# Turning gathered expert rows by transposing DMAs instead of TensorE transposes

## The chip, the cores and the metric

The kernel runs on one core of a Trainium2 chip. The metric is the device time of one execution, in microseconds. Engines are called TensorE (PE in the rows, PEld for its weight loads), VectorE (DVE), ScalarE (ACT), GpSimd (POOL) and SyncE (SP, whose queue issues plain DMAs). Each has its own queue of instructions, worked off in order, and they meet only through semaphores.

## The reference

Input x is (8, 1024, 256) in float32. An attention layer comes first, then a layer of 16 experts in which each expert picks its 1024 best tokens (expert choice), plus a shared expert:

```python
x = x + layernorm(attention(layernorm(x)))
h = layernorm(x)                                 # 8192 rows of 256
scores = softmax(h @ gate_w.T).T                 # 16 x 8192
topk_weight, topk_idx = top_k(scores, 1024)
xg = h[topk_idx]                                 # 16 x 1024 x 256, gathered rows
hid = gelu(xg @ Wg.T) * (xg @ Wu.T)              # 1024 hidden values
eo = (hid @ Wd.T) * topk_weight                  # scattered back by addition
shared = (gelu(h @ Sg.T) * (h @ Su.T)) @ Sd.T    # 512 hidden values, all rows
x = x + layernorm(scatter_add(eo) + shared)
```

## The kernel before, in words

After the attention (the first 615 us) all of the expert layer is one list of blocks of 512 rows, which every engine goes through in the same order (schedule, L1377). Blocks 0 to 11 are three quarters of the shared expert's rows, blocks 12 to 43 (E0 = 12, D0 = 44) are the 16 experts with two blocks each (tb = 0 and tb = 1, called even and odd here), and the last four are the rest of the shared expert.

An expert block has 8 steps (one for each 128 hidden values) and a down-projection. In a step TensorE does 12 matmuls of 512 columns (up, L1426): gate and up, two halves of the 256 features, each as three products of high and low parts (mm3, L57), since float32 values are split into two parts for the fast matmul. The order is

```python
for it in range(2, its[b]): step(b, it)
for it in range(2): step(b + 1, it)
down(b)
```

so step 0 of block b+1 follows step 7 of block b at once, and the down-projection of b (32 matmuls of 512 and 32 of 256 columns, 11.2 us) comes after step 1 of b+1.

What other engines do in a step: ScalarE (step, L1609) waits for TensorE's step, computes the gelu into HF (L1614), copies the high part of the hidden values of the step before (part_hi, L1578), and where there is one a quarter of a weight's high part (w_hi, L1555; wd in steps 4 to 7 of even blocks, the next expert's wg and wu in all steps of odd ones). VectorE (step, L1799) multiplies HF by the up-projection (L1802), then makes the low parts: of the hidden values (part_lo, L1723), of the weight (w_lo, L1712). In even blocks it also sums and centers rows of wd (L1746, L87) in steps 2 to 4. TensorE's step s waits until the product of step s-2 is done (s_mul). PSUM and HF have two buffers.

The input of a block is XT[b % 2], turned (features on partitions) and split into high and low part, each in two halves dk of 128 features. TensorE waits ahead of step 0 of block b for both low halves of it:

```python
if it == 0:
    wait(pe, s_xlo, 2 * (b + 1))
wait(pe, s_mul, s - 1)
```

For expert blocks x comes from gathered rows: GpSimd issues 8 indirect DMAs for each expert (gather, L2055; 128 rows each) into XG[n % 2], rows on partitions. TensorE turns the rows of block b+1 in steps 3 and 4 of block b, one half dk each with 4 transposes into PSUM (turn_part, L1412, L1423; semaphore s_xt). In the same steps, behind the weight, ScalarE takes the high part out of PSUM (x_hi, L1557, L1572) and VectorE the low part (x_lo, L1714, L1718; semaphore s_xlo). The first expert block is turned whole in step 3 of the last shared block. s_xt also tells GpSimd and SyncE when XG may be written again.

Of the kernel before, what the change touches and what calls it, by code (L numbers as in the profile page):

```python
# [23 lines left out]
F32 = mybir.dt.float32  # L24
F32R = mybir.dt.float32r
BF16 = mybir.dt.bfloat16
I32 = mybir.dt.int32
ALU = mybir.AluOpType
ACT = mybir.ActivationFunctionType
# [4 lines left out]
P = 128  # L34
E = 16
# [1231 lines left out]
def moe(nc, io, c):  # L1267
# [7 lines left out]
    with ExitStack() as ctx:  # L1275
# [46 lines left out]
        cm = new("cm", [P, NI])  # L1322

        def tile(u, t):
            b, first, _ = WHERE[u]
            return F[b][:, first + t, :]
# [22 lines left out]
        s_hlo2, s_evd = sem("s_hlo2"), sem("s_evd")  # L1349
        s_f = {u: sem(f"s_f_{u}") for u in ("d0", "d1", "e0", "e1", "e2", "e3", "e4", "e5", "b7")}  # L1350
        s_cen, s_sqv, s_sqa, s_r, s_pc, s_n, s_o = (sem(n) for n in ("s_cen", "s_sqv", "s_sqa", "s_r", "s_pc", "s_n", "s_o"))
# [3 lines left out]
        tail = Tail(io, c, sem, new, psG, psU, psX, psD)  # L1355
        tail.s_ev_down0, tail.ev_down0 = s_ev, EV0 + 4
# [46 lines left out]
        def _(pe):  # L1403
            def turn(b):

                n, tb = expert(b)
                q = n % 2
                wait(pe, s_ga[q][tb], 64 * (n // 2 + 1))
                for dk in range(KD):
                    turn_part(b, dk)  # L1410

            def turn_part(b, dk):  # L1412

                n, tb = expert(b)
                q = n % 2
                if dk == 0:
                    wait(pe, s_ga[q][tb], 64 * (n // 2 + 1))
                if b > E0:
                    wait(pe, s_xlo, 2 * (b - 1) + dk + 1)
                else:  # L1420
                    wait(pe, topk.s_acc, AHEAD)
                for t in range(4):
                    i = pe.transpose(psX[:, dk, t * P:(t + 1) * P], XG[q][:, 4 * tb + t, dk * P:(dk + 1) * P], c.ident[:, :])  # L1423
                i.then_inc(s_xt, 1)

# [10 lines left out]
            def step(b, it):  # L1436
                s = base[b] + it
                if is_b(b) and s % 4 == 3:
                    topk.sum(pe, s - 1.5 - SHIFT)
                if is_b(b):  # L1440
                    tail.p_begin(pe, s)
                if is_e(b):
                    n, tb = expert(b)
                    if tb == 0 and it % 2 == 0:
                        for w in "gu":
                            wait(pe, s_wlo[w], 4 * n + it // 2 + 1)
                if b == D0 and it == 0:
                    pe.wait_ge(s_dlo, 3)
# [4 lines that stand above are left out]
                def middle():  # L1453
                    if is_b(b):
                        if s % 4 == 0:
                            topk.sum(pe, s - 2 - SHIFT)
                        topk.tensor_at(pe, s - 0.25 - SHIFT)
                        tail.p_middle(pe, s)
                        if b == E0 - 1 and it == 3:
                            turn(E0)  # L1460

                if is_b(b):
                    up(it, XT[b % 2], (bsw["g"], bsw["u"]), middle)
                    topk.tensor_at(pe, s - SHIFT)
                    tail.p_end(pe, s)
                elif is_e(b):
                    up(it, XT[b % 2], (wg[n % 2], wu[n % 2]), middle)
                    if it in (3, 4) and is_e(b + 1):
                        turn_part(b + 1, it - 3)
                    if it == 6 and 0 <= b - 1 - E0 < NCH - AHEAD:  # L1470
                        topk.p_list(pe, AHEAD + b - 1 - E0)
                else:
                    up(it, XT[b % 2], (dsw["g"], dsw["u"]), middle)
# [65 lines left out]
        def _(a):  # L1539
# [17 lines left out]
            def x_hi(b, dk):  # L1557
                dst = XT[b % 2][0][:, dk, :]
                if is_b(b):
                    src = XR[b % 2][:, dk, :]  # L1560
                    if dk == 0:
                        wait(a, s_xr[b % 2], 16 * (b // 2 + 1))
                elif is_e(b):
                    src = psX[:, dk, :]
                    wait(a, s_xt, 2 * (b - E0) + dk + 1)
# [23 lines left out]
            def squares(u, ts):  # L1589

                for t in ts:
                    if u in ("d2", "d3"):
                        wait(a, s_evd, 4 * int(u[1]) + t + 1)
                    else:
                        wait(a, s_f[u], 16)
                    z = BASE[u] + t
# [12 lines left out]
            def step(b, it):  # L1609
# [7 lines left out]
                if is_b(b):  # L1617
# [90 lines left out]
        def _(v):  # L1708
# [5 lines left out]
            def x_lo(b, dk):  # L1714
                hi, lo = (t[:, dk, :] for t in XT[b % 2])
                src = XR[b % 2][:, dk, :] if is_b(b) else psX[:, dk, :] if is_e(b) else XRD[b - D0][:, dk, :]
                wait(v, s_xhi, 2 * b + dk + 1)
                v.tensor_tensor(lo, src, hi.bitcast(F32), ALU.subtract).then_inc(s_xlo, 1)  # L1718

            def part_lo(b, it):  # L1720
# [40 lines left out]
            def squares(u, ts):  # L1761

                if u[0] == "e":
                    wait(v, s_f[u], 16)
                v.drain()
# [33 lines left out]
            def step(b, it):  # L1799
# [16 lines left out]
                elif is_e(b):  # L1816
# [116 lines left out]
        def _(sp):  # L1933
# [68 lines left out]
            load_shared("d")  # L2002
            sp.wait_ge(s_xt, 4 * (E - 1))
            sp.wait_ge(s_tw, E - 1)
# [10 lines left out]
            load_shared("u")  # L2015
            sp.wait_ge(s_xt, 4 * E)
            sp.wait_ge(s_tw, E)
# [31 lines left out]
        def _(g):  # L2049
# [83 lines left out]
            part_lo(1, 1)  # L2133
            g.wait_ge(s_sqa, 1)
            chain(0)
# [17 lines left out]
            g.wait_ge(s_sqv, 6)  # L2153
            g.wait_ge(s_sqa, 2)
            chain(4)
            part_lo(3, 3)
            store("e2")
            g.wait_ge(s_sqa, 3)
            chain(5)
            g.wait_ge(s_sqa, 4)  # L2160
            chain(6)
# [68 lines left out]
```

## Time and profile before

| | us |
|---|---|
| median of 3 runs | 2064.74 |
| lowest, highest | 2063.34, 2065.69 |
| the profiled execution | 2064.56 |
| its span in the profile | 2062.6 |
| TensorE busy in the span | 2022.0 (98%) |
| VectorE, ScalarE, GpSimd busy | 1320.0, 970.5, 511.6 |

The span goes from the first to the last instruction of the profile. An engine's row in a timeline gives the start, the length and, in square brackets, how long the engine had been idle before it and what it had waited for. Lengths of neighbours overlap, as the engines are pipelined; what an instruction costs its queue is the distance from start to start.

### The profile page before, as it was taken

To read this page: it belongs to the slowest core of one execution; us is meant where nothing else is said; L and a number is where in the kernel's file an instruction comes from. 1 tells how busy PE (TensorE), PEld (TensorE's weight loads), DVE (VectorE), ACT (ScalarE), POOL (GpSimd) and SP (SyncE) were. 2 spreads that over 40 slices of the span, in tenths; PEclk is the share of its full clock that TensorE was granted. 3 is DMA by queue.
4 is the path that set the end of the run, shared out by engine and by line. 5 is a ranking of instruction groups with operands and counts; after the bars stand their busy time and mean duration, and the time that the engine had idled before them with its cause. 6 is when DMAs were issued, how large, how long until landed. Compare 5 with 4: busy or idle time off the path is not lost.

```text
span 2062.6 us, 30183 instructions
## 1 busy us (share of the span) xinstructions
PE 2022.0 (98%) x11290; PEld 1724.4 (84%) x11290; DVE 1320.0 (64%) x2489; ACT 970.5 (47%) x1840; POOL 511.6 (25%) x604
## 2 busy tenths in 40 slices
PE   7999999999999999999999999999999999999996
PEld 6888888888888888888888888888888888888885
DVE  6676686676667678666656666655555555555647
ACT  4564574564554444444434344444444444444444
POOL 0021022022021000314223332333233323322246
PEclk9999999999999999999999999999999999999998
DMA  3011111111015211333333333333332333234466
GB/s 115 1 42 43 62 63 42 61 62 46 38 68 191 84 62 52 98 81 65 91 63 74 78 71 83 81 74 72 83 83 73 70 85 83 73 70 116 105 211 163
DMA packets 56395, 163.96 MB, mean 79 GB/s; under 512 B 9552, under 2 KB 26064, under 8 KB 49104
## 3 DMA queue, kind: packets, MB, share of 16 engines
q1 hardware_dynamic: 30880, 124.55, 16.7%
q0 software_dynamic: 25392, 37.77, 11.5%
q8 instruction: 78, 1.28, 0.3%
q14 instruction: 45, 0.37, 0.1%
HBM read 102.97 MB, written 59.31 MB: 79 GB/s over the span
## 4 chain that ended last, share of the span: by engine, by line
PE 67%; DVE 2%; ACT 0%; DMA 0%; DVEq 0%; issue 0%; SPq 0%; ACTq 0%
PE mo_psD L1502 11%; PE mo_psG L59 7%; PE mo_psU L59 7%; PE mo_psU L60 7%; PE mo_psU L61 7%; PE mo_psG L61 7%; PE mo_psG L60 7%; PE mo_psD L1504 6%; PE mo_psD L59 2%; PE mo_psD L61 1%; PE mo_psD L60 1%; PE mo_psX L1423 1%; PE mo_psX L1228 1%; DVE mo_junk_v L1768 0%; DVE mo_HF L1802 0%; DMA X1a<-wd_in 0%
## 5 line engine op out<-in xcount | busy, mean ns | idle before, releaser
L1614 ACT ACTIVATE mo_HF<-mo_psG 128x512 f32<-128x512 f32 x320 | 191.3, 598 | 466.6 <-PE mo_psU L61 437.1
L1802 DVE TENSOR_TENSOR mo_HF<-mo_psU,mo_HF 128x512 f32<-128x512 f32 x320 | 220.6, 689 | 282.7 <-ACT mo_HF L1614 280.4
L2081 POOL DMA_INDIRECT ACC<-OUT,mo_GI x128 | 202.6, 1583 | 674.5 <-DVE OUT L1884 666.1
L1502 PE MATMUL mo_psD<-wd,mo_H_hi 128*128 128x512 f32 x1024 | 360.9, 393 | 0.2 <-DVE OUT L1884 0.2
L1504 PE MATMUL mo_psD<-wd,mo_H_lo 128*128 128x256 f32 x1024 | 289.4, 283 | 0.0
L59 PE MATMUL mo_psG<-mo_XT_hi,wg_hi 128*128 128x512 f32 x640 | 261.1, 408 | 2.3 <-DVE mo_HF L1802 1.8
L59 PE MATMUL mo_psU<-mo_XT_hi,wu_hi 128*128 128x512 f32 x640 | 253.3, 396 | 0.0
L61 PE MATMUL mo_psG<-mo_XT_hi,wg_lo 128*128 128x512 f32 x640 | 252.8, 395 | 0.0
L60 PE MATMUL mo_psU<-mo_XT_lo,wu_hi 128*128 128x512 f32 x640 | 252.6, 395 | 0.0
L61 PE MATMUL mo_psU<-mo_XT_hi,wu_lo 128*128 128x512 f32 x640 | 252.4, 394 | 0.0
L60 PE MATMUL mo_psG<-mo_XT_lo,wg_hi 128*128 128x512 f32 x640 | 252.3, 394 | 0.0
L1502 PEld LDWEIGHTS mo_psD<-wd,mo_H_hi 128*128 128x128 f32 x1024 | 192.3, 188 | 44.9 <-DVE OUT L1884 0.5
L1723 DVE TENSOR_TENSOR mo_H_lo<-mo_HF,mo_H_hi 128x512 fp32r<-128x512 f32 x304 | 207.7, 683 | 0.0
L1578 ACT ACTIVATE mo_H_hi<-mo_HF 128x512 fp32r<-128x512 f32 x318 | 198.5, 624 | 9.3 <-DVE mo_HF L1802 9.3
L1884 DVE SCALAR_TENSOR_TENSOR OUT<-mo_psD,mo_TW,OUT 128x256 f32<-128x256 f32 x128 | 62.0, 484 | 214.8 <-ACT OUT L1673 214.8
L1504 PEld LDWEIGHTS mo_psD<-wd,mo_H_lo 128*128 128x128 f32 x1024 | 192.5, 188 | 1.5
L1673 ACT ACTIVATE OUT<-mo_psD,mo_TW 128x256 f32<-128x256 f32 x128 | 60.8, 475 | 268.9 <-PE mo_psD L1504 268.9
L59 PEld LDWEIGHTS mo_psG<-mo_XT_hi,wg_hi 128*128 128x128 f32 x640 | 120.6, 188 | 28.8 <-DVE mo_HF L1802 3.4
L61 PEld LDWEIGHTS mo_psG<-mo_XT_hi,wg_lo 128*128 128x128 f32 x640 | 120.4, 188 | 28.4
L61 PEld LDWEIGHTS mo_psU<-mo_XT_hi,wu_lo 128*128 128x128 f32 x640 | 120.5, 188 | 28.1
L60 PEld LDWEIGHTS mo_psU<-mo_XT_lo,wu_hi 128*128 128x128 f32 x640 | 120.5, 188 | 28.0
L59 PEld LDWEIGHTS mo_psU<-mo_XT_hi,wu_hi 128*128 128x128 f32 x640 | 120.6, 188 | 27.8
(304 smaller groups left out, 4182.8 us busy)
## 6 DMA issues: line engine op xcount, KB each, us to landing
X1a<-wg_in SPq DMA_DIRECT2D x16, 1024.0 KB, 4.8
X1a<-wu_in SPq DMA_DIRECT2D x16, 1024.0 KB, 4.8
X1a<-wd_in SPq DMA_DIRECT2D x16, 1024.0 KB, 4.9
XN<-XG SPq DMA_DIRECT2D x8, 1088.0 KB, 4.1
X<-x_in SPq DMA_DIRECT2D x8, 1024.0 KB, 6.4
out_dram<-X SPq DMA_DIRECT2D x8, 1024.0 KB, 4.7
XN2T<-xn2T SPq DMA_DIRECT2D x8, 1024.0 KB, 3.9
mo_F<-ACC SPq DMA_DIRECT2D x7, 1024.0 KB, 12.0
```

The costliest lines, as they stand in the source:

```text
L59: pe.matmul(out, w_hi, x_hi, start=first, stop=False)
L60: pe.matmul(out, w_hi, x_lo, start=False, stop=False)
L61: return pe.matmul(out, w_lo, x_hi, start=False, stop=last)
L1502: pe.matmul(psD[:, t % 2, :], h_hi, wd_both[:, it, :, :].rearrange("p z d -> p (z d)"), start=(it == 0), stop=False)
L1504: i = pe.matmul(psD[:, t % 2, 0:D], h_lo, wd[0][:, it, :], start=False, stop=(it == n - 1))
L1578: a.activation(hidden(b, it)[0], HF[:, it % 2, :], ACT.Copy).then_inc(s_hhi, 1)
L1614: a.activation(HF[:, it % 2, :], psG[:, it % 2, :], ACT.Gelu).then_inc(s_gelu, 1)
L1673: i = a.activation(OUT[:, t, :], psD[:, t % 2, 0:D], ACT.Copy, scale=scale)
L1723: v.tensor_tensor(lo, HF[:, it % 2, :], hi.bitcast(F32), ALU.subtract).then_inc(s_hlo, 1)
L1802: v.tensor_tensor(HF[:, it % 2, :], psU[:, it % 2, :], HF[:, it % 2, :], ALU.mult).then_inc(s_mul, 1)
L1884: v.scalar_tensor_tensor(OUT[:, t, :], psD[:, t % 2, D:2 * D], TW[n % 2][:, 4 * tb + t:4 * tb + t + 1], OUT[:, t, :], ALU.mult, ALU.add).t ...
L2081: g.indirect_dma_start(out=io["ACC"], out_offset=bass.IndirectOffsetOnAxis(ap=GI[n % 2][:, 4 * tb + t:4 * tb + t + 1], axis=0), in_=OUT[:, ...
```

## The change

The transposes of gathered rows on TensorE go, except for the first expert block (turn_first). For every other expert block b+1 the work is done while block b runs:

- steps 0 and 1, ScalarE (split_rows): the 32-bit values are read as pairs of 16-bit integers, and the lower halves (step 0) and the upper halves (step 1) of the block's rows are copied to a new tile halves, 1024 elements per partition each;
- step 2, ScalarE's queue (turn_rows): one DMA with transpose turns all of halves (512 KB, 16 blocks of 128 x 128) into a new tile turned, semaphore s_tt;
- step 5, VectorE (join_rows): two copies put the turned halves together again as 32-bit values in XTF, which lies over halves;
- steps 6 and 7 instead of 3 and 4: ScalarE and VectorE split x into high and low part (x_hi, x_lo), now from XTF.

The waits of GpSimd and SyncE for free gather tiles go by the split (s_half2) instead of the transposes. Two semaphores are shared with later uses (s_f of e0, s_sqa), and small tiles of the stage between attention and experts lie in turned.

```diff
+        halves, turned = new("halves", [P, 2, KD, 4, P], U16), new("turned", [P, 2, KD * 4 * P], U16)
+        XTF = mem.over("XTF", [P, KD, 512], F32, "halves", 0)
@@ TensorE
                     up(it, XT[b % 2], (wg[n % 2], wu[n % 2]), middle)
-                    if it in (3, 4) and is_e(b + 1):
-                        turn_part(b + 1, it - 3)
@@ ScalarE
+            def split_rows(b, z):
+                n, tb = expert(b)
+                q = n % 2
+                if z == 0:
+                    wait(a, s_ga[q][tb], 64 * (n // 2 + 1))
+                    wait(a, s_xlo, 2 * b)
+                rows = XG[q][:, 4 * tb:4 * tb + 4, 0:D].bitcast(U16).rearrange("p t (k d z) -> p z k t d", k=KD, z=2)
+                i = a.activation(halves[:, z, :, :, :], rows[:, z, :, :, :], ACT.Copy)
+                if z == 1:
+                    i.then_inc(s_half2, 1)
+
+            def turn_rows(b):
+                wait(a, s_half2, b - E0)
+                a.dma_start(out=turned[:, :, :].rearrange("p z (m t) -> p (z m) t", t=P),
+                            in_=halves[:, :, :, :, :].rearrange("p z k t d -> p (z k t d)"), transpose=True).then_inc(s_tt, 16)
...
                 elif is_e(b):
+                    if it < 2 and is_e(b + 1):
+                        split_rows(b + 1, it)
+                    if it == 2 and is_e(b + 1):
+                        turn_rows(b + 1)
                     task = weight_task(b, it)
                     if task:
                         w_hi(*task)
...
-                    if it in (3, 4):
-                        x_hi(b + 1, it - 3)
+                    if it in (6, 7):
+                        x_hi(b + 1, it - 6)
@@ VectorE
+            def join_rows(b):
+                wait(v, s_tt, 16 * (b - E0))
+                words = XTF[:, :, :].rearrange("p k t -> p (k t)").bitcast(U16).rearrange("p (n z) -> p z n", z=2)
+                for z in range(2):
+                    i = v.tensor_copy(words[:, z, :], turned[:, z, :])
+                i.then_inc(s_xt, 1)
...
-                    if it in (3, 4):
-                        x_lo(b + 1, it - 3)
-                        if it == 4 and b < D0 - 1 and expert(b)[1]:
-                            scores_of(expert(b)[0] + 1)
+                    if it == 5 and is_e(b + 1):
+                        join_rows(b + 1)
+                    if it in (6, 7):
+                        x_lo(b + 1, it - 6)
+                    if it == 4 and b < D0 - 1 and expert(b)[1]:
+                        scores_of(expert(b)[0] + 1)
@@ GpSimd, gather(n)
-                wait(g, s_xt, 4 * (n - 1))
+                wait(g, s_half2, 2 * (n - 1) - 1)
```

## Rows read from the trace of the kernel before

**Rows 1.** Busy time by stretch: window, length, PE, PEld, DVE, ACT, POOL (count), PEclk, DMA, GB/s.

```profile
1400.00:1600.00 200.00, 200.00 (x977) 166.62 (x976) 114.55 (x181) 87.70 (x165) 60.71 (x49) 1.00 0.33 79
```

**Rows 2.** Line L1423, one of two equal groups: ns min/median/max, first and last start.

```profile
L1423 PE MATMUL mo_psX<-ident,mo_XG x128: 270/272/300, 847.7 to 1852.9; 128*128 128x128 f32 x128
```

**Rows 3.** Timeline of ScalarE, steps 4 to 6 of an odd expert block.

```profile
1473.96 0.60 ACT L1614 ACTIVATE mo_HF<-mo_psG 128x512 f32<-128x512 f32 x1 [1.11 <-PE mo_psU L61]
1474.46 0.62 ACT L1578 ACTIVATE mo_H_hi<-mo_HF 128x512 fp32r<-128x512 f32 x1
1474.98 0.62 ACT L1555 ACTIVATE wu_hi<-X1a 128x512 fp32r<-128x512 f32 x1
1475.50 0.59 ACT L1572 ACTIVATE mo_XT_hi<-mo_psX 128x512 fp32r<-128x512 f32 x1
1477.20 0.60 ACT L1614 ACTIVATE mo_HF<-mo_psG 128x512 f32<-128x512 f32 x1 [1.11 <-PE mo_psU L61]
...
1479.99 0.60 ACT L1614 ACTIVATE mo_HF<-mo_psG 128x512 f32<-128x512 f32 x1 [1.16 <-PE mo_psU L61]
```

**Rows 4.** Timeline of VectorE in the first of these steps.

```profile
1474.60 0.69 DVE L1802 TENSOR_TENSOR mo_HF<-mo_psU,mo_HF 128x512 f32<-128x512 f32 x1 [0.74 <-ACT mo_HF L1614]
...
1475.80 0.68 DVE L1712 TENSOR_TENSOR wu_lo<-X1a,wu_hi 128x512 fp32r<-128x512 f32 x1
1476.40 0.68 DVE L1718 TENSOR_TENSOR mo_XT_lo<-mo_psX,mo_XT_hi 128x512 fp32r<-128x512 f32 x1
```

**Rows 5.** Timeline of TensorE: the first matmul of the next step.

```profile
1477.00 0.39 PE L59 MATMUL mo_psG<-mo_XT_hi,wg_hi 128*128 128x512 f32 x1
```

**Rows 6.** Timelines of VectorE and TensorE where the first expert block begins.

```profile
849.03 1.29 DVE L1718 TENSOR_TENSOR mo_XT_lo<-mo_psX,mo_XT_hi 128x512 fp32r<-128x512 f32 x2 [0.44 <-ACT mo_XT_hi L1572]
...
850.58 0.47 PE L59 MATMUL mo_psG<-mo_XT_hi,wg_hi 128*128 128x512 f32 x1 [0.38 <-DVE mo_XT_lo L1718]
```

**Rows 7.** Timeline of TensorE: three instructions behind idle gaps.

```profile
14.39 0.86 PE L284 MATMUL psS<-ident,X1a 128*128 128x128 f32 x3 [3.39 <-ACT X1a L412]
...
657.93 1.09 PE L766 MATMUL mo_psX<-ident,XG 128*128 128x128 f32 x8 [1.67 <-ACT XG L832]
...
2038.13 0.39 PE L59 MATMUL mo_psD<-wg_hi,mo_H_hi 128*128 128x256 f32 x1 [2.11 <-DVE mo_F L1777]
```

**Rows 8.** Busy time by stretch, behind these gaps (columns as in rows 1).

```profile
14.45:17.75 3.30, 3.30 (x15) 2.95 (x16) 1.44 (x3) 3.30 (x6) 0.00 (x0) 0.50 0.46 189
...
658.00:661.00 3.00, 3.00 (x21) 2.69 (x22) 1.29 (x2) 1.43 (x4) 0.00 (x0) 1.00 0.00 1
...
2038.50:2041.85 3.35, 3.35 (x19) 3.35 (x18) 2.47 (x6) 2.42 (x9) 3.02 (x6) 0.50 0.01 1
```

**Rows 9.** Timeline of TensorE in the last of them: two matmuls, eleven between them.

```profile
2039.06 0.41 PE L61 MATMUL mo_psD<-wg_hi,mo_H_lo 128*128 128x256 f32 x1
...
2041.62 0.41 PE L61 MATMUL mo_psD<-wg_hi,mo_H_lo 128*128 128x256 f32 x1
```

**Rows 10.** Groups by line and shape: busy us, mean ns of one, idle before.

```profile
L87 DVE SCALAR_TENSOR_TENSOR X1a<-mo_cm,X1a 128x1024 f32<-128x1024 f32 x33 | 40.4, 1224 | 1.7
...
L1587 ACT ACTIVATE wg_hi<-X1a 128x1024 fp32r<-128x1024 f32 x2 | 2.1, 1049 | 0.0
```

**Rows 11.** Timeline of VectorE: a one-input copy of 512 elements.

```profile
12.05 0.42 DVE L152 CAST m<-xn2T 128x512 fp32r<-128x512 f32 x1
```

**Rows 12.** DMA issues: count, KB each (none for gathers), us from issue to landing.

```profile
ACC<-OUT SPq DMA_DIRECT2D x12, 512.0 KB, 3.0
...
XG<-XN,mo_GI POOLq DMA_INDIRECT x64, 2.8
...
xn2T<-sd_in SPq DMA_DIRECT2D x1, 512.0 KB, 9.1
```

**Rows 13.** Line L1943 on SyncE's queue: ns of an issue.

```profile
L1943 SPq DMA_DIRECT2D ACC<-OUT x12: 319/327/381, 652.5 to 862.5; - x12
```

**Rows 14.** Timeline of GpSimd: the fourth gather of an expert.

```profile
1441.29 0.95 POOL L2070 DMA_INDIRECT XG<-XN,mo_GI  x1 [0.31 <-issue]
```

More of the change, by code:

```diff
@@ L27 @@
 I32 = mybir.dt.int32
+U16 = mybir.dt.uint16
 ALU = mybir.AluOpType
@@ L1349, in moe @@
         s_hlo2, s_evd = sem("s_hlo2"), sem("s_evd")
-        s_f = {u: sem(f"s_f_{u}") for u in ("d0", "d1", "e0", "e1", "e2", "e3", "e4", "e5", "b7")}
-        s_cen, s_sqv, s_sqa, s_r, s_pc, s_n, s_o = (sem(n) for n in ("s_cen", "s_sqv", "s_sqa", "s_r", "s_pc", "s_n", "s_o"))
+        TURNED = 2 * E - 1
+        s_half2, s_tt = sem("s_half2"), sem("s_tt")
+        s_f = {u: sem(f"s_f_{u}") for u in ("d0", "d1", "e1", "e2", "e3", "e4", "e5", "b7")} | {"e0": s_tt}
+        s_sqa, SQA0, landed = s_half2, TURNED, lambda u: 16 * (TURNED + 1) if u == "e0" else 16
+        s_cen, s_sqv, s_r, s_pc, s_n, s_o = (sem(n) for n in ("s_cen", "s_sqv", "s_r", "s_pc", "s_n", "s_o"))
         s_x1 = {b: sem(f"s_x1_{b}") for b in (3, 4, 5, 6, 7)}
@@ L1354, in moe @@
         s_pass = sem("s_pass")
-        tail = Tail(io, c, sem, new, psG, psU, psX, psD)
+        tail = Tail(io, c, sem, Over(mem, "turned", 4096), psG, psU, psX, psD)
         tail.s_ev_down0, tail.ev_down0 = s_ev, EV0 + 4
@@ L1403, in _, with turn_first @@
         def _(pe):
[L1404 to L1408, printed above, removed]
+            def turn_first():
+                wait(pe, s_ga[0][0], 64)
+                wait(pe, topk.s_acc, AHEAD)
                 for dk in range(KD):
[L1410 to L1424, printed above, removed]
+                    for t in range(4):
+                        i = pe.transpose(psX[:, dk, t * P:(t + 1) * P], XG[0][:, t, dk * P:(dk + 1) * P], c.ident[:, :])
+                    i.then_inc(s_xt, 1)
             def up(it, x, ws, middle):
@@ L1459, in middle @@
                         if b == E0 - 1 and it == 3:
-                            turn(E0)
+                            turn_first()
                 if is_b(b):
@@ L1563, in x_hi @@
                 elif is_e(b):
-                    src = psX[:, dk, :]
-                    wait(a, s_xt, 2 * (b - E0) + dk + 1)
+                    src = (psX if b == E0 else XTF)[:, dk, :]
+                    wait(a, s_xt, dk + 1 if b == E0 else 2 + b - E0)
                 else:
@@ L1594, in squares @@
                     else:
-                        wait(a, s_f[u], 16)
+                        wait(a, s_f[u], landed(u))
                     z = BASE[u] + t
@@ L1715, in x_lo @@
                 hi, lo = (t[:, dk, :] for t in XT[b % 2])
-                src = XR[b % 2][:, dk, :] if is_b(b) else psX[:, dk, :] if is_e(b) else XRD[b - D0][:, dk, :]
+                src = XR[b % 2][:, dk, :] if is_b(b) else (psX if b == E0 else XTF)[:, dk, :] if is_e(b) else XRD[b - D0][:, dk, :]
                 wait(v, s_xhi, 2 * b + dk + 1)
                 v.tensor_tensor(lo, src, hi.bitcast(F32), ALU.subtract).then_inc(s_xlo, 1)
+            def join_rows(b):
[3 more added lines that the diff above has]
+                    i = v.tensor_copy(words[:, z, :], turned[:, z, :])
+                i.then_inc(s_xt, 1)
             def part_lo(b, it):
@@ L1763, in squares @@
                 if u[0] == "e":
-                    wait(v, s_f[u], 16)
+                    wait(v, s_f[u], landed(u))
                 v.drain()
@@ L2002, in _ @@
             load_shared("d")
-            sp.wait_ge(s_xt, 4 * (E - 1))
+            sp.wait_ge(s_half2, 2 * (E - 1) - 1)
             sp.wait_ge(s_tw, E - 1)
@@ L2015, in _ @@
             load_shared("u")
-            sp.wait_ge(s_xt, 4 * E)
+            sp.wait_ge(s_half2, 2 * E - 1)
             sp.wait_ge(s_tw, E)
@@ L2133, in _ @@
             part_lo(1, 1)
-            g.wait_ge(s_sqa, 1)
+            g.wait_ge(s_sqa, SQA0 + 1)
             chain(0)
@@ L2153, in _ @@
             g.wait_ge(s_sqv, 6)
-            g.wait_ge(s_sqa, 2)
+            g.wait_ge(s_sqa, SQA0 + 2)
             chain(4)
@@ L2157, in _ @@
             store("e2")
-            g.wait_ge(s_sqa, 3)
+            g.wait_ge(s_sqa, SQA0 + 3)
             chain(5)
-            g.wait_ge(s_sqa, 4)
+            g.wait_ge(s_sqa, SQA0 + 4)
             chain(6)
```

## Prediction

> **What bounds the kernel now.** I read first the busy time by stretch, then the places of the line that the change removes, then the timelines of one expert block, and last the idle gaps of TensorE with the clock after them. In the stretch of the experts TensorE is busy 200.00 us of 200 at full clock, with VectorE at 115 and ScalarE at 88 [rows 1]. So whatever TensorE no longer does comes off the time one for one, and whatever TensorE newly waits for goes on it one for one. The other engines matter only where they hand over to TensorE.
>
> A step of a block (12 matmuls of up-projection) goes like this. TensorE ends the step; ScalarE starts the gelu, then copies the high part of the step before, then a quarter of a weight, then, in steps 3 and 4, the high part of x for the next block [rows 3]. VectorE starts its product 0.64 us after the gelu's start, and its instructions follow at 0.60 us each: product, low part of H, low part of the weight, low part of x, which ends at 1476.40 + 0.68 = 1477.08, 3.12 us after the gelu's start at 1473.96 [rows 3, 4]. The reader is to keep these 3.12 us in mind. They are longer than a step, and they do no harm in steps 3 and 4, because x is wanted only when step 0 of the next block begins, three steps later.
>
> **What is removed.** A step with four transposes behind it lasts 1477.20 - 1473.96 = 3.24 us, one without 1479.99 - 1477.20 = 2.79 us [rows 3], so four transposes cost 0.45 us of TensorE (the 272 ns of each in [rows 2] overlap). There are 256 of them in two such groups; 8 (the first block's) stay, 248 go: 62 x 0.45 = 27.9 us off.
>
> **What is moved, the term that decides.** x is split into its parts in steps 6 and 7 instead of 3 and 4. All engines run the same order: step 7 of block b is followed at once by step 0 of block b+1, and the down-projection of b comes only after step 1. Step 0 waits on TensorE for s_xlo of both halves. The second half is now made in step 7: on ScalarE behind the gelu of step 7, which itself waits for TensorE to finish step 7; on VectorE behind product, low part of H and low part of the weight. So TensorE finishes step 7 and then waits for the whole chain of 3.12 us. The next step's first matmul starts now 0.20 us ahead of the gelu (1477.00 and 1477.20) [rows 3, 5]. From the end of x's low part to the first matmul it takes 0.25 us, seen where the first expert block does just this (849.03 + 1.29 = 850.32 to 850.58, with TensorE idle for it) [rows 6]; I add 0.08 for that first matmul's slower start, about the difference between its length and that of the others (0.47 against 0.39) [rows 5, 6]. Sum: 0.20 + 3.12 + 0.25 + 0.08 = 3.65 us for each hand-over. Every expert block has one, 32 in all; in the last there is no weight to split, one VectorE instruction of 0.60 less. 31 x 3.65 + 3.05 = 116.2 us on. It can't be hidden: the matmuls that could fill it stand behind the waiting one in TensorE's queue.
>
> **The clock after such a gap.** TensorE has in this trace an idle gap of 3.39 us and one of 2.11 us [rows 7]. After each the granted clock was 0.50 (1.2 GHz) for a stretch that I can fill with a window of 3.3 us (the edges make it about 3.4); after a gap of 1.67 us it stayed at 1.00 (2.4 GHz) [rows 7, 8]. At the low level 12 matmuls of 256 columns took 2041.62 - 2039.06 = 2.56 us, 0.213 each [rows 9], so one of 512 columns some 0.427 (estimate: twice that) against 2.79 / 12 = 0.233 now. 3.4 us at that rate lose 3.4 x (1 - 0.233 / 0.427) = 1.54 us. The new gap, about 3.5 us idle, is as long as the longest of those, so I take the drop each time: 32 x 1.54 = 49.3 us on.
>
> **What is added.** Split on ScalarE, two instructions of 1024 elements for each block, in steps 0 and 1: nearest row 1.05 us [rows 10], about 0.1 of it overlapped as with the others. ScalarE's step is at most 3 x 0.52 = 1.56 us there; with 0.95 it is 2.5 of 2.79, so it stays hidden. It needs gathered rows earlier than before: the fourth gather is issued at 1441.29, in step 4 [rows 14], its rows are wanted from step 0 of the next block, some 9.8 us later, and gathers land in 2.8 us [rows 12]. Zero.
>
> The transposing DMA, issued in step 2 by ScalarE behind its copy (1.04 us after the gelu). Nothing in the trace transposes by DMA. Its issue: the plain issues of SP are 0.33 us each [rows 13]; on ScalarE that is hidden, and so would be anything up to about 1.2 us (the idle rest of the step) plus 1.5 (product done 1.33 after the gelu's start, wanted at 2.79). Beyond 2.7 us every further microsecond stalls TensorE; I take 0, and 9 us (0.3 in 31 blocks) as the upper end. Its landing: 512 KB of plain DMA take 3.0 to 9.1 us [rows 12]. VectorE wants it at step 5 after three instructions, 3 x 2.79 + 0.64 + 1.80 = 10.8 us after step 2's gelu, 9.8 us after the issue. Both ends fit, so 0, with little room above 9.1. Queued behind it on ScalarE is one weight copy in odd blocks; SP's and POOL's queues are not passed by it. The wait stands in VectorE's queue, with product 6 behind it.
>
> The join on VectorE, two copies of 1024 elements of 16 bits, written at every second place. A copy of 512 fp32 takes 0.42 us [rows 11] where a two-input instruction takes 0.68 [rows 4], so one-input copies go faster; at that rate 1024 elements are some 0.6 of queue time, at the slow rate 1.15 (1.22 for 1024 elements [rows 10]). Step 5 then holds 1.8 + 1.2 = 3.0 us (or 4.1). The excess over 2.79 is used up in step 6 at the fast rate, except in even blocks, where sums and centering in steps 2 to 4 leave VectorE about 0.3 behind: 0.12 us in 16 blocks, 2 us. At the slow rate some 0.95 us more in each hand-over: 29 us, the upper end; below zero nothing speaks for. I take the fast one. The Trainium skill, "VectorE: DVE Perf Modes", section "What auto-detection actually checks", says the same: one source and destination in SBUF get two results per cycle without step 1 being asked, which would make 2 us of this and not 29.
>
> **The sum**, against the profiled execution's 2064.56 us (span 2062.6, 2.0 around it; the median of the runs is 2064.74, so the difference doesn't matter): 2064.6 - 27.9 + 116.2 + 49.3 + 2 = 2204.2 us.
>
> **Rivals.**
> *The clock holds.* A gap of 1.67 us did not lower it; after the two others it fell. If it holds after most of the new gaps: 2204.2 - 49.3 = 2155. For it: only that every new gap has full work on both sides. Against: so had the gap of 2.11.
> *The DMA is late.* If 16 blocks of 128 x 128 are turned one after another, or in pieces so small that they cost more than plain rows, it lands after the 9.8 us, and each microsecond over is one more in each of 31 hand-overs: 2 us late 2266, 3 late 2297. For it: unknown operation and only 0.7 us between the slowest plain row and the limit. Against: the typical 512 KB are 3 to 5 us. The Trainium skill, "VectorE: DVE Perf Modes", section "The three transpose paths", gives 1309 ns for one 128 x 128 by DMA and advises TensorE where PSUM will do; sixteen in a row would be 20.9 us by it, 11.1 late, 2204 + 344 = 2548. "Advanced Engine Details and Errata", section "X-Bar Transpose (TRN2)", has such DMAs as fast as plain ones, which leaves my sum as it is. No row here decides between the two pages.
> *Not slower: the hand-over is covered.* If x's low part were ready when TensorE ends step 7, only the removal would count: 2064.6 - 27.9 = 2037. The point from which it decides is a hand-over under 0.9 us (27.9 / 31). It would take work of TensorE between step 7 and the wait, such as the down-projection; the order in the code puts that two steps later.
>
> **Chances.** Forecast with its own range of 2190 to 2245: 0.60. Clock holds (wholly or in part, 2150 to 2190): 0.14. DMA late: 0.20, half of it under 2300. Not slower: 0.02. Others, like collisions of copies of VectorE with GpSimd's gathers: 0.04. The range 2150 to 2300 leaves out about 0.15. A measurement of this kernel tells some 0.2% (4 us) from no change; faster 0.02, same 0.01, slower 0.97.
>
> **What would show it.** TensorE idle some 3.5 us ahead of step 0 of every expert block, released by VectorE's low part of x (L1718 of before); TensorE's busy share in the stretch of the experts down to nine tenths; granted clock 0.50 for 3.4 us in each block; steps 3 and 4 at 2.79 us. If the DMA is late, VectorE is idle ahead of the join, released by the DMA. I am wrong if TensorE's gap is released by something else, or if no gap stands ahead of step 0.

## The result, and the profile after

| | before | after |
|---|---|---|
| median (lowest to highest), us | 2064.04 (2062.87 to 2065.69) | 2208.82 (2204.11 to 2214.57) |
| span of the profiled execution, us | 2062.6 | 2206.4 |
| mean granted clock of TensorE | 0.995 | 0.968 |

Four runs each, on the same chip. The changed kernel takes 1.0702 times as long (95% interval 1.0675 to 1.0729), 145 us more. The forecast was 2204.2.

The page of the changed kernel: the span, the busy time, the queue of the transposing DMAs, the chain that ended last.

```profile
span 2206.4 us, 29842 instructions
PE 2053.5 (93%) x11042; PEld 1733.3 (79%) x11042; DVE 1360.7 (62%) x2551; ACT 1033.5 (47%) x1902; POOL 521.5 (24%) x604
...
q10 hardware_dynamic: 64480, 16.26, 3.6%
...
PE 55%; DVE 13%; ACT 1%; issue 1%; POOL 1%; DVEq 0%; DMA 0%; SPq 0%; ACTq 0%; POOLq 0%
```

The chain is where to look first. VectorE now has 13% of it, and DMA 0%. The packets of the transposing DMAs (q10) took 3.6% of the 16 DMA engines' time, and the time went to waits for VectorE. The same stretch of the experts as in [rows 1]:

```profile
1400.00:1600.00 200.00, 179.84 (x805) 147.16 (x806) 105.44 (x165) 84.52 (x149) 59.54 (x47) 0.93 0.36 82
```

TensorE is busy 180 us of 200, at a mean clock of 0.93. What it waits for (us in all, times, longest):

```profile
PE mo_psG L60 <- DVE mo_XT_lo L1731: 109.9, 32, 4.3
...
PE mo_psG L60 <- issue: 2.7, 1, 2.7
```

One wait ahead of step 0 of every expert block, released by the low part of x, as forecast. The second line is one of the same hand-overs, whose releaser the profile doesn't show. The first line also holds the 0.38 us that [rows 6] had. So 32 new gaps hold 109.9 + 2.7 - 0.4 = 112.2 us, 3.5 each.

The timelines of TensorE at the end of an even block and of the odd one behind it, and of VectorE in the last step of the odd one:

```profile
1515.11 0.40 PE L62 MATMUL mo_psU<-mo_XT_hi,wu_lo 128*128 128x512 f32 x1
1519.35 0.80 PE L60 MATMUL mo_psG<-mo_XT_hi,wg_hi 128*128 128x512 f32 x1 [3.84 <-DVE mo_XT_lo L1731]
...
1555.16 0.40 PE L62 MATMUL mo_psU<-mo_XT_hi,wu_lo 128*128 128x512 f32 x1
1558.98 0.76 PE L60 MATMUL mo_psG<-mo_XT_hi,wg_hi 128*128 128x512 f32 x1 [3.42 <-DVE mo_XT_lo L1731]
```

```profile
1556.23 0.69 DVE L1823 TENSOR_TENSOR mo_HF<-mo_psU,mo_HF 128x512 f32<-128x512 f32 x1
1556.84 0.68 DVE L1744 TENSOR_TENSOR mo_H_lo<-mo_HF,mo_H_hi 128x512 fp32r<-128x512 f32 x1
1557.43 0.69 DVE L1725 TENSOR_TENSOR wu_lo<-X1a,wu_hi 128x512 fp32r<-128x512 f32 x1
1558.04 0.69 DVE L1731 TENSOR_TENSOR mo_XT_lo<-mo_XTF,mo_XT_hi 128x512 fp32r<-128x512 f32 x1
```

These are the four instructions of [rows 4], product to low part of x, with the same lengths; the gelu ahead of them starts at 1555.60. In [rows 3 to 5] TensorE worked on beside them; here it stands. From the start of the last matmul to that of the next is 3.82 us in the odd block and 4.24 in the even one. 0.23 of that is the usual distance, so these two hand-overs cost 3.59 and 4.01 us. All odd ones but the last are like this one (TensorE idle for 3.4 us). The even ones are of two kinds. In the nine blocks behind the seventh expert TensorE is idle for 3.7 to 3.9 us, but in the first seven experts for only 3.2, except behind the very first block, where it is 4.3.

The clock, in windows through these two gaps (PEclk is the third number from the right):

```profile
1517.50:1518.00 0.50, 0.00 (x0) 0.00 (x0) 0.50 (x1) 0.40 (x1) 0.00 (x0) 0.50 0.45 87
...
1524.50:1525.00 0.50, 0.50 (x4) 0.41 (x3) 0.00 (x0) 0.33 (x1) 0.00 (x0) 1.00 0.00 0
...
1557.50:1558.00 0.50, 0.00 (x0) 0.00 (x0) 0.50 (x2) 0.25 (x1) 0.00 (x0) 1.00 0.00 0
1558.00:1558.50 0.50, 0.00 (x0) 0.00 (x0) 0.50 (x2) 0.00 (x0) 0.00 (x0) 0.90 0.00 0
1558.50:1559.00 0.50, 0.02 (x1) 0.05 (x1) 0.22 (x1) 0.00 (x0) 0.00 (x0) 0.50 0.00 0
...
1561.50:1562.00 0.50, 0.50 (x3) 0.36 (x3) 0.00 (x0) 0.00 (x0) 0.00 (x0) 0.68 0.91 344
1562.00:1562.50 0.50, 0.50 (x4) 0.42 (x3) 0.00 (x0) 0.00 (x0) 0.00 (x0) 1.00 0.36 148
```

Here the clock falls to 0.50 (1.2 GHz) inside the gap, not at its end, and comes back in the odd block 2.8 us after the work does (at about 1561.8). In the even block it stays low until 1524.3 or so. Over all expert blocks, I count 28 low stretches at 32 gaps. 19 of them begin inside the gap, nine up to 1.5 us after its end, and behind four gaps (two of 3.21 and two of 3.42 us) there is none. Ten are 6.8 us long, the others 3.4. The low stretches add up to 129.7 us, and TensorE was busy for 108.3 of these, which by the predicted rate, 1 - 0.233 / 0.427 = 0.454, is 49 us lost. The rate itself is borne out: behind the even gap the second to the seventh matmul start at 1519.94 to 1522.07, 0.426 us apart.

One thing is new. ScalarE's issue of the transposing DMA (timeline of ScalarE in step 2 of an odd block):

```profile
1541.48 0.60 ACT L1623 ACTIVATE mo_HF<-mo_psG 128x512 f32<-128x512 f32 x1 [2.31 <-PE mo_psU L62]
1541.49 3.37 ACTq L1580 DMA_TRANSPOSE mo_turned<-mo_halves  x1
1541.98 0.63 ACT L1587 ACTIVATE mo_H_hi<-mo_HF 128x512 fp32r<-128x512 f32 x1
1544.90 0.63 ACT L1547 ACTIVATE wg_hi<-X1a 128x512 fp32r<-128x512 f32 x1 [2.30 <-issue]
1545.44 0.58 ACT L1623 ACTIVATE mo_HF<-mo_psG 128x512 f32<-128x512 f32 x1
...
1552.80 0.60 ACT L1623 ACTIVATE mo_HF<-mo_psG 128x512 f32<-128x512 f32 x1 [1.15 <-PE mo_psU L62]
```

```profile
L1580 ACTq DMA_TRANSPOSE mo_turned<-mo_halves x31: 1333/3326/3415, 865.9 to 2051.1; - x31
```

The issue holds ScalarE's queue for 3.3 us at the median, ten times the 0.33 of a plain one [rows 13]. The next gelu starts 3.96 us after this one. By step 6 almost all of it has been made up: 1552.80 - 1541.48 = 11.32 us for four steps, against 4 x 2.79 = 11.16.

The whole: the span grew by 143.8 us. Transposes -27.9; hand-overs 112.2 idle and 0.17 in each for the restart (3.59 - 3.42), 117.6; clock 49; ScalarE's issue 0.16 in 15 odd blocks, 2.4. Together 141; the other 2.7 us have no place here.

### The profile page after: what moved, and what is told of

Same layout as the page of the kernel before. It is cut to its first block, busy times and chain, and to the rows that moved or that the text cites. A ratio compares the mean times of both kernels' runs of the same rounds, so it can differ in the third digit from the quotient of the medians.

```text
span 2206.4 us, 29842 instructions
## 1 busy us (share of the span) xinstructions
PE 2053.5 (93%) x11042; PEld 1733.3 (79%) x11042; DVE 1360.7 (62%) x2551; ACT 1033.5 (47%) x1902; POOL 521.5 (24%) x604
## 4 chain that ended last, share of the span: by engine, by line
PE 55%; DVE 13%; ACT 1%; issue 1%; POOL 1%; DVEq 0%; DMA 0%; SPq 0%; ACTq 0%; POOLq 0%
PE mo_psD L1494 11%; PE mo_psG L60 6%; PE mo_psG L62 6%; PE mo_psG L61 6%; PE mo_psU L60 6%; PE mo_psD L1496 5%; PE mo_psU L61 5%; PE mo_psU L62 5%; DVE mo_HF L1823 3%; DVE mo_H_lo L1744 3%; DVE mo_XT_lo L1731 2%; PE mo_psD L60 1%; PE mo_psD L62 1%; PE mo_psD L61 1%; DVE wd L1725 1%; DVE X1a L88 1%
## 5 line engine op out<-in xcount | busy, mean ns | idle before, releaser
L60 PE MATMUL mo_psG<-mo_XT_hi,wg_hi 128*128 128x512 f32 x640 | 272.6, 426 | 115.3 <-DVE mo_XT_lo L1731 109.9
L62 PE MATMUL mo_psG<-mo_XT_hi,wg_lo 128*128 128x512 f32 x640 | 264.5, 413 | 0.0
L61 PE MATMUL mo_psG<-mo_XT_lo,wg_hi 128*128 128x512 f32 x640 | 264.1, 413 | 0.0
L60 PE MATMUL mo_psU<-mo_XT_hi,wu_hi 128*128 128x512 f32 x640 | 262.8, 411 | 0.0
L61 PE MATMUL mo_psU<-mo_XT_lo,wu_hi 128*128 128x512 f32 x640 | 260.0, 406 | 0.0
L62 PE MATMUL mo_psU<-mo_XT_hi,wu_lo 128*128 128x512 f32 x640 | 258.5, 404 | 0.0
L60 PEld LDWEIGHTS mo_psG<-mo_XT_hi,wg_hi 128*128 128x128 f32 x640 | 127.3, 199 | 161.8 <-DVE mo_XT_lo L1731 65.2
L62 PEld LDWEIGHTS mo_psG<-mo_XT_hi,wg_lo 128*128 128x128 f32 x640 | 127.4, 199 | 30.7
L60 PEld LDWEIGHTS mo_psU<-mo_XT_hi,wu_hi 128*128 128x128 f32 x640 | 126.7, 198 | 30.1
L61 PEld LDWEIGHTS mo_psU<-mo_XT_lo,wu_hi 128*128 128x128 f32 x640 | 126.7, 198 | 30.2
```

What stands on the lines that cost most here:

```text
L60: pe.matmul(out, w_hi, x_hi, start=first, stop=False)
L61: pe.matmul(out, w_hi, x_lo, start=False, stop=False)
L62: return pe.matmul(out, w_lo, x_hi, start=False, stop=last)
```

## The experiments

The kernel before was run beside each on the same chip, at medians between 2064.7 and 2069.0; ratios are to it. Experiments on different chips can differ by these 4 us without a reason in the kernel.

**e1_move: the kernel before, x split in steps 6 and 7 in 18 blocks, nothing else.** Transposes stay.

```diff
-                    if it in (3, 4):
-                        x_hi(b + 1, it - 3)
+                    if it in ((6, 7) if b >= E0 + 14 else (3, 4)):
+                        x_hi(b + 1, it % 3 if b >= E0 + 14 else it - 3)
```

(The same for x_lo.)

> The kernel before, with all TensorE transposes and without any DMA transpose, split or join; only the high and low parts of x are made in steps 6 and 7 instead of 3 and 4, for blocks from E0+14 on (18 hand-overs, the last without a weight). Theory (the hand-over behind step 7 is what costs): 17 x 3.65 + 3.05 = 65.1 us of waiting and 18 x 1.54 = 27.7 us of low clock, so 2064 + 93 = 2157 us, with TensorE idle 3.4 to 3.9 us ahead of step 0 of these blocks alone. Rival (the added work or the DMA costs, the place of x does not): 2064 us.

Measured: 2164.25 us, ratio 1.0482 (1.0461 to 1.0503), 99.5 us more. TensorE's waits:

```profile
PE mo_psG L59 <- DVE mo_XT_lo L1718: 56.6, 18, 3.4
...
1464.05 0.80 PE L59 MATMUL mo_psG<-mo_XT_hi,wg_hi 128*128 128x512 f32 x1 [3.21 <-DVE mo_XT_lo L1718]
```

The move alone makes the gaps: 3.42 us in odd blocks, as in the changed kernel, and 3.21 in even ones, as in its first seven experts. With the last one (2.7 us) and without the 0.4 of [rows 6], 18 gaps hold 58.9 us, and with 0.17 each for the restart the hand-overs cost 62 us. TensorE worked for 79.9 us at the low clock, x 0.454 = 36.3. Together that is 98 of the 99.5 us. The clock's share was expected at 27.7: here, too, half of the low stretches (9 of 17) were twice as long as taken. No DMA, no split and no join is needed for the loss. The rival, a cause in the new work, falls.

**e2_work: the changed kernel with all of its new work, but x split in steps 3 and 4, straight from the gathered, unturned rows.** The experts' values are therefore others; every instruction and DMA is there.

```diff
-                    if it in (6, 7):
-                        x_hi(b + 1, it - 6)
+                    if it in (3, 4):
+                        x_hi(b + 1, it - 3)
```

(The same for x_lo; both read XG instead of XTF.)

> The changed kernel with all of its new work (split, transposing DMA, join, no TensorE transposes), but x is split in steps 3 and 4 as before, out of the rows that were gathered and not turned; so the values of the experts are not the reference's and the hand-over is early. Theory: only the removal counts, 2064 - 27.9 = 2036 us, up to 2046 with what ScalarE's queue loses by the issues of 3.3 us; no idle gap ahead of step 0 and the granted clock full. Rival (the DMA, the copies or the queue of ScalarE are what costs in the changed kernel): over 2064 us, up to 2209.

Measured: 2050.5 us, ratio 0.9934 (0.9918 to 0.9951). It is faster, so the new work isn't what costs, and the clock never falls in the expert blocks. But it gains 14 us where the removal should give 28. TensorE's waits, and VectorE from step 4 to the start of step 5 of an even block:

```profile
PE mo_psG L60 <- DVE mo_HF L1834: 7.7, 22, 1.0
```

```profile
1498.20 0.68 DVE L1834 TENSOR_TENSOR mo_HF<-mo_psU,mo_HF 128x512 f32<-128x512 f32 x1
1498.80 0.68 DVE L1755 TENSOR_TENSOR mo_H_lo<-mo_HF,mo_H_hi 128x512 fp32r<-128x512 f32 x1
1499.40 1.22 DVE L88 SCALAR_TENSOR_TENSOR X1a<-mo_cm,X1a 128x1024 f32<-128x1024 f32 x1
1500.53 0.69 DVE L1736 TENSOR_TENSOR wd<-X1a,wd 128x512 fp32r<-128x512 f32 x1
1501.14 0.68 DVE L1742 TENSOR_TENSOR mo_XT_lo<-XG,mo_XT_hi 128x512 fp32r<-128x512 f32 x1
1501.74 0.68 DVE L1834 TENSOR_TENSOR mo_HF<-mo_psU,mo_HF 128x512 f32<-128x512 f32 x1
```

From the product at 1498.20 to the next at 1501.74 VectorE has 3.54 us of work without a pause, for a step of 2.79. While TensorE had transposes the step was 3.24 [rows 3], so they hid most of this. In the even blocks behind the seventh expert VectorE now sets the pace: nine of them last 34.6 us, 1.1 more than without any wait. That is 10 us, and with 0.16 us for the issue in 15 odd blocks 12 to 13 of the 14 that are missing. In the first seven experts an even block lasts 34.9 us, of which the choice of tokens is 1.3 on TensorE, so nothing is lost there.

**e8_join7: e2_work with the join of even blocks in step 7 instead of 5.**

> The run with the whole new work but x split in steps 3 and 4 from unturned rows, now with the join of even blocks in step 7 instead of step 5 (the values of the experts are not the reference's, as there). Theory: that run gained only half of the 27.9 us since in even blocks VectorE had centering, the low part of x and the join close behind one another, and its low parts came late for TensorE by 0.2 to 0.4 us some forty times; with the join two steps later it has caught up before, the waits on HF go (7.7 us there in 22) and the time is 2036 to 2043 us. Rival: what is missing is TensorE's own (the steps without transposes are not 0.45 us shorter, or the new instructions slow others by sharing memory); then the time stays at 2048 to 2053.

Measured: 2057.86 us, ratio 0.9949 (0.9935 to 0.9962), 11 us less than before and no better than e2_work: a miss. TensorE's waits on HF are still 7.7 us, now in 16. The block lengths tell more than the total. These are the gelus of step 2, ScalarE's timeline, of e2_work and then of e8_join7, each at the ends of an odd and an even block late in the stretch:

```profile
1457.30 0.60 ACT L1634 ACTIVATE mo_HF<-mo_psG 128x512 f32<-128x512 f32 x1 [2.31 <-PE mo_psU L62]
...
1490.98 0.60 ACT L1634 ACTIVATE mo_HF<-mo_psG 128x512 f32<-128x512 f32 x1 [2.31 <-PE mo_psU L62]
...
1525.62 0.60 ACT L1634 ACTIVATE mo_HF<-mo_psG 128x512 f32<-128x512 f32 x1 [2.32 <-PE mo_psU L62]
```

```profile
1465.54 0.60 ACT L1634 ACTIVATE mo_HF<-mo_psG 128x512 f32<-128x512 f32 x1 [2.31 <-issue]
...
1499.28 0.60 ACT L1634 ACTIVATE mo_HF<-mo_psG 128x512 f32<-128x512 f32 x1 [2.31 <-issue]
...
1533.48 0.60 ACT L1634 ACTIVATE mo_HF<-mo_psG 128x512 f32<-128x512 f32 x1 [2.30 <-issue]
```

A block without any wait is 8 x 2.79 + 11.2 = 33.5 us. The odd block is 33.7 in both. The even one is 34.64 in e2_work and 34.20 in e8_join7. So the join in step 5 causes 0.4 us of the 1.1 that an even block loses here. The other 0.7 I put down to centering and x's low part in the same steps; that was not tried alone. In the first seven experts, where TensorE and VectorE also work on the choice of tokens, a pair of blocks took 70.7 us on the mean with the join in step 7 and 69.9 with it in step 5. Why it costs more there is open; it eats the gain.

**e3_join4_x56: the changed kernel with the join in step 4 and x in steps 5 and 6.** The DMA stays in step 2.

```diff
-                    if it == 5 and is_e(b + 1):
+                    if it == 4 and is_e(b + 1):
                         join_rows(b + 1)
-                    if it in (6, 7):
-                        x_lo(b + 1, it - 6)
+                    if it in (5, 6):
+                        x_lo(b + 1, it - 5)
```

> The changed kernel with the join in step 4 and x split in steps 5 and 6. Theory: the low part of x ends 3.12 us after the gelu of step 6, one step of 2.79 earlier than now, so odd blocks keep a hand-over of 3.65 - 2.79 = 0.86 us; in even blocks sums and centering put VectorE 1.3 us behind, 2.1 us, and some 0.2 us in step 4: 16 x 0.86 + 16 x 2.3 = 51 us, so 2064 - 27.9 + 51 = 2087 us, and with a low clock after the longer ones up to 2112. The DMA must land 7 us after its issue; where it is later VectorE idles ahead of the join. Rival (the DMA is just in time and step 5 was needed): over 2150 us.

Measured: 2080.29 us, ratio 1.0078 (1.0061 to 1.0094). One step earlier takes away 129 of the 145 us.

```profile
PE mo_psG L60 <- DVE mo_XT_lo L1731: 26.9, 26, 1.4
...
PE mo_psG L60 <- DVE mo_HF L1823: 8.3, 13, 1.6
```

The gaps are at most 1.6 us, and behind none of them does the clock fall in the expert blocks. That is how the two terms hang together: a step less of lateness (2.79 us) takes the clock's term away with it. The rival (the DMA just in time) falls too.

**e4_fill: the changed kernel with 12 more matmuls ahead of each of the 32 waits**, on old data into a PSUM tile that nothing reads.

```diff
                 if it == 0:
+                    if E0 < b <= D0:
+                        h = XT[(b - 1) % 2][0]
+                        for _ in range(12):
+                            pe.matmul(psX[:, 1, :], h[:, 0, 0:P], h[:, 1, :], start=True, stop=True)
                     wait(pe, s_xlo, 2 * (b + 1))
```

> The changed kernel with 12 more matmuls of 512 columns ahead of TensorE's wait in each of the 32 hand-overs (into a free PSUM bank, nobody reads them; 12 x 0.233 = 2.8 us, less than the gap of 3.4 to 3.9). Theory (the low clock follows the idle gap and is worth 49 us): the clock stays full in the experts and the time falls to 2209 - 49 = 2160 us in spite of more matmuls. Rival (the waiting alone costs, the clock's stretches are for free or come for another reason): 2209 us or more.

Measured: 2157.61 us, ratio 1.0448 (1.0431 to 1.0466), 51 us faster than the changed kernel with more work in it. The filler and the step behind it:

```profile
1530.67 2.92 PE L1447 MATMUL mo_psX<-mo_XT_hi 128*128 128x512 f32 x12
...
1534.05 0.50 PE L60 MATMUL mo_psG<-mo_XT_hi,wg_hi 128*128 128x512 f32 x1 [0.46 <-DVE mo_XT_lo L1735]
```

The clock stays full in the expert blocks, and the gap is filled. The hand-over is nearly as late as before: in even blocks it is the same, in odd ones 0.2 us shorter (3.38 instead of 3.58), since the first matmul starts 0.06 us after x's low part instead of 0.26. Why it does so is not shown. That makes 3 us in all, so some 48 of the 51 us are the clock's (predicted 49.3), and 2158 is near what the rival "the clock holds" gave (2155).

**e5_issue4: the changed kernel with the DMA issued in step 4 instead of 2.** It was meant to measure how much room the DMA's landing has.

```diff
-                    if it == 2 and is_e(b + 1):
+                    if it == 4 and is_e(b + 1):
                         turn_rows(b + 1)
```

> The changed kernel with the transposing DMA issued in step 4 instead of 2, so that the join in step 5 must wait for it and shows when it lands. The issue holds ScalarE's queue 3.3 us from the start of the step; the join is wanted 5.2 us after it. Theory (it lands 2 to 3 us after its issue's end, like the fastest plain transfer): 0.1 to 1.1 us of waiting, 2209 to 2240 us. Rival (it lands only about 9.8 us after, just in time as it stands): 4.6 us each, over 2300 us.

Measured: 2273.03 us, ratio 1.0989 (1.0969 to 1.1009), between the two expectations. VectorE waited 3.8 us in all for the DMAs, four times, so nearly all land in time even so. What was lost begins on ScalarE's queue:

```profile
PE mo_psG L60 <- DVE mo_HF L1823: 29.6, 18, 3.0
...
L1580 ACTq DMA_TRANSPOSE mo_turned<-mo_halves x31: 1332/3044/7410, 879.3 to 2125.0; - x31
...
1501.54 0.33 SPq L1974 DMA_DIRECT2D X1a<-wd_in  x1
...
1501.75 5.40 ACTq L1580 DMA_TRANSPOSE mo_turned<-mo_halves  x1
...
1507.25 0.63 ACT L1547 ACTIVATE wu_hi<-X1a 128x512 fp32r<-128x512 f32 x1 [4.40 <-issue]
```

In odd blocks SyncE issues a load of 1 MB 0.2 us ahead, and ScalarE's issue then takes 5.4 us. The gelu behind it is late, and TensorE waits for the product: 29.6 us, where it was 2.7 in the changed kernel. Its waits for x's low part grow too, from 109.9 to 126.9 us, and its work at the low clock from 108 to 150 us, which at 0.454 is 19 us more. These three make 63 of the 64 us. Whether the load is the cause, e7_issue3 and e9_load_after ask.

**e7_issue3: as e5_issue4, but in step 3 in odd blocks**, one step ahead of the load.

> The changed kernel with the transposing DMA issued in step 4 of even blocks, as in the run that issued it in step 4 of all, but in step 3 of odd ones. Theory: the issue was 5.4 us long in odd blocks because SyncE issues a weight load of 1 MB in step 4 of them, 0.2 us ahead (both issue descriptors and move data at the same time); one step earlier, with no load beside it, the issue is 3.4 us at most, VectorE's and ScalarE's lags of odd blocks go, and the time is 2209 to 2235 us. Rival: the length comes from something else in the late part of an odd block (the instructions of ScalarE's own queue, the state of its ring); the issue stays at 5.3 us or so in odd blocks and the time stays above 2255.

Measured: 2220.48 us, ratio 1.0744 (1.0725 to 1.0763). No issue is longer than 3.2 us, and in odd blocks they are 1.8 to 2.7:

```profile
L1580 ACTq DMA_TRANSPOSE mo_turned<-mo_halves x31: 1333/1808/3184, 879.2 to 2068.6; - x31
```

The time is within the theory's range, but the issue also moved by a step, so the load isn't yet singled out. The run stays 12 us above the changed kernel, though its issues are shorter and its waits for x's low part the same (110.8 us): TensorE worked for 128 us at the low clock instead of 108, which is 9 us.

**e6_early: a version that keeps what the change removes and avoids what it moves.** The first four expert blocks are turned by TensorE as before. The other 28 are split, turned and joined a block earlier: the rows are split in steps 5 and 6 (6 and 7) of the block before last, turned in step 7 or in step 0 behind it, joined in step 3 of odd blocks and step 1 of even ones, and x is split in step 4 (odd) and step 5 (even).

```diff
+        def x_at(b, it):
+            if b + 1 < TE or b + 1 == D0:
+                return (it - 3,) if it in (3, 4) else ()
+            return range(KD) if it == (4 if expert(b)[1] else 5) else ()
...
+                        if it == 0 and b + 1 >= TE and is_e(b + 1):
+                            turn_rows(b + 1)
+                        if it == 7 and b + 2 >= TE and is_e(b + 2):
+                            turn_rows(b + 2)
```

> The DMA's way for 28 blocks (the first four by TensorE as before), started a block earlier: for blocks tb = 0 split in steps 6 and 7 two blocks ahead, issue in step 0, join in step 3, x in step 4; for blocks tb = 1 split in steps 5 and 6, issue in step 7, join in step 1, x in step 5. No hand-over waits. Theory: 28 x 0.9 = 25 us off, some 0.16 us lost to each issue on ScalarE's queue (4.5 us): 2064 - 20.5 = 2043 us. Rival (the issue of 3.3 us on ScalarE's queue stalls TensorE by more than the transposes cost): 2064 us or more.

Measured: 2050.78 us, ratio 0.9913 (0.9900 to 0.9927): faster than before by 0.9%, about 18 of the 25 us that 28 blocks can give. TensorE's waits for the low part of x are down to one of 1.8 us. What is missing is again an issue beside a load, every fourth one:

```profile
1451.76 0.33 SPq L1991 DMA_DIRECT2D X1a<-wu_in  x1
...
1451.92 5.50 ACTq L1593 DMA_TRANSPOSE mo_turned<-mo_halves  x1
...
1457.52 0.60 ACT L1636 ACTIVATE mo_HF<-mo_psG 128x512 f32<-128x512 f32 x1 [4.06 <-issue]
```

Here the load alone doesn't explain it. Two blocks away the same load is issued 0.2 us ahead of a transposing DMA whose issue takes 1.33 us.

**e9_load_after: e6_early, with SyncE loading wu only when that DMA has landed.**

```diff
+                    if n >= 1:
+                        wait(sp, s_tt, 16 * (2 * n - 1))
                     load_w("u", n + 1)
```

> The version with DMAs started a block earlier, with one wait more: SyncE loads the up-projection weights of the next expert only when the transposing DMA that ScalarE issues in step 0 of the odd block has landed. In that version every other one of these issues began 0.2 us behind the issue of the 1 MB load and was 5.3 to 5.8 us long, the ones between them 1.33 us long beside the same load. Theory: the long ones come from the load beside them; they fall to 2 us or so, ScalarE no longer comes late with a gelu (5.5 us steps go), about 9 us come back, and the time is 2038 to 2045 us. Rival: the length is a matter of which issue of the series it is, and not of the load: they stay above 5 us and the time at 2048 to 2053.

Measured: 2044.84 us, ratio 0.9883 (0.9866 to 0.9899): 1.2% faster than before, the best of all versions. Its issues, their landing, and the stretch of the experts:

```profile
L1593 ACTq DMA_TRANSPOSE mo_turned<-mo_halves x28: 1332/1838/1993, 962.0 to 1879.0; - x28
...
DMA to landing us min/median/max: 4.2/4.3/6.1
```

```profile
1400.00:1600.00 200.00, 200.00 (x957) 166.58 (x957) 122.12 (x194) 100.87 (x179) 65.79 (x51) 1.00 0.43 96
```

The issues of 5.3 to 5.8 us became 1.8 to 1.9, in the same place of the same order, with the load taken from beside them. That shows the load beside them as their cause (whether its issue or its data does it was not tried). The gain over the kernel before grew from 17.5 to 23.7 of the 25 us that 28 blocks can give. That about every fourth issue is 1.3 to 1.6 us, with or without a load, is seen in all traces and not explained. In this stretch TensorE is again busy 200 us of 200, with full clock and no transposes.

## Why the prediction was right, step by step

**What bounds the kernel, and the removal.** In the changed kernel steps 3 and 4 last 2.79 us, so the 27.9 us do come off there. But "comes off one for one" holds only while VectorE keeps up: in e2_work 10 of the 28 us went to its steps of 3.5 us in even blocks. The prediction should have looked at VectorE's sum over the steps that got shorter. It didn't matter for the total, as x's low part had left those steps.

**The hand-over.** 3.65 us predicted with the slower start, 3.59 measured in odd blocks, and e1_move shows that the move alone does it. That the sum of all hand-overs comes out at 117.6 us against 118.2 (116.2 + 2) is partly luck, as two errors cancel in even blocks. The first: from the end of x's low part to the first matmul I took the 0.25 us of [rows 6]. Odd blocks have 0.26, even ones 0.05 us. Without any lag of VectorE an even hand-over costs 3.38 us, as in e1_move and in the first seven experts: 16 x 0.27 = 4.3 us less than taken. The second: the lag that I put at 0.12 us was none in six of the first seven even blocks and 0.63 (4.01 - 3.38) in the nine late ones, where VectorE was still behind when step 7 ended; with block 12 (1.1 us) that is 6.8 us against 2. The two copies of the join cost 1.28 to 1.33 of queue time instead of 1.2, and e1_move, which has no join and keeps the longer steps with transposes, has no lag in the same blocks. How much of the lag comes from the join and how much from the shorter steps, with sums and centering in them, was not tried.

**The clock.** Total 49 by the trace and 48 by e4_fill, 49.3 predicted. That the clock falls at these gaps and what work costs at its low level were right (0.427 us for a matmul predicted, 0.426 measured), but that the totals agree so closely is luck, made of errors that cancel. I had 32 drops of 3.4 us, all of it beside work, 108.8 us. There were 28; 21 us of them (129.7 - 108.3) lie in the gaps themselves, where a low clock costs nothing; and ten were twice as long. The rows of before could carry the rate at the low level and that the clock falls with such gaps, but not the length. The gap of 2.11 us that I also went by was a weak sign: the same gap at that place is followed by a low stretch in five of the eleven traces and by none in the others.

**The split.** As predicted, hidden: 1.05 us an instruction, no wait of TensorE for it.

**The DMA's issue.** The step mis-sized most: 0.33 us by [rows 13], 3.33 measured. I had written that TensorE feels it beyond 2.7 us, and 0.6 us over that point cost 0.16 us a block in odd blocks, 2.4 in all, because the late gelus catch up by step 6. It stayed inside the upper end of 9. Placed beside a load it costs far more (e5_issue4 took 64 us more than the changed kernel, and e7_issue3 only 12 more).

**The DMA's landing.** No wait of VectorE for it in the changed kernel, against a limit of 9.8 us. Its own trace has no landing times; the median is 4.8 us in e2_work and e3_join4_x56 and 4.3 in e9_load_after. In e2_work and e3_join4_x56 the very first one, issued 1.5 us behind a weight load, is the longest, with 8.3 and 10.6 us, and no wait followed. The rival "DMA is late" falls. The Trainium skill, "VectorE: DVE Perf Modes", section "The three transpose paths", gives 1309 ns for one 128 x 128 block; sixteen in a row would by an estimate from it be 20.9 us, and the landings of 4.3 and 4.8 us don't bear that out. The Trainium skill, "Advanced Engine Details and Errata", section "X-Bar Transpose (TRN2)", has such DMAs as fast as plain ones; the landings agree with it, as plain 512 KB took 3.0 to 9.1 us [rows 12].

**The join.** 732 to 887 ns a copy, overlapped to 1.28 to 1.33 for two: near the fast rate (1.2), far from the slow one (2.3).

**Not slower.** It needed a hand-over under 0.9 us. In e3_join4_x56 the gaps are near that (26.9 us in 26), and the time is within 1% of before.

**The whole.** Measured were 2208.8 us against 2204.2. The path, the wait and its releaser were as forecast. The nearness of the total owes something to luck, in even hand-overs and in the clock; the 4.6 us between them are about the 2.4 of the issue, taken as 0, and the 2.7 that stay open.

## What to carry to other kernels

Before moving a producer, count from the event that starts its chain to its consumer's first use: a chain of 3.1 us is free three steps ahead and costs all of itself one step ahead. TensorE paid for gaps of 3.2 us and more a second time in its clock (some 1.5 us each on the mean), and for gaps of up to 1.6 us it did not, so shortening such a gap gave back more than its own length. When an operation leaves the bounding engine, the steps get shorter for all others too: add up the next engine over just these steps.

## What the runs showed of the hardware

- A transposing DMA of 512 KB (16 blocks of 128 x 128 x 2, 2080 packets) lands in 4.3 to 4.8 us at the median (three traces; up to 6.1 in e9_load_after, 10.6 at the most), but its issue holds the issuing engine's queue: 1.3 to 1.6 us about every fourth time, 1.8 to 2.0 in e9_load_after, 3.3 at the median in the changed kernel (why not 1.8 was not tried), 5.3 to 7.4 with a load of 1 MB issued 0.2 us ahead. Delaying that load brought 5.5 down to 1.85.
- TensorE's clock fell inside a gap of 3.4 us while nothing ran; of 28 falls in the changed kernel 19 were inside the gap and nine up to 1.5 us behind it. Gaps of up to 1.6 us did not lower it, one of 2.1 us near the end of the kernel did in five traces of eleven, and those of 3.2 to 4.3 us in the changed kernel did in 27 cases of 31. Some low stretches were 6.8 us and the others 3.4; what decides between them I could not tell.
- A 16-bit copy of 1024 elements, written at every second place, takes VectorE 0.64 to 0.67 us of queue time (two of them 1.28 to 1.33).
